# Local attention, norms and gated layers in one block with waits by unit and bank, and retention in rounds of eight heads

## The reference

```
x = x + 0.5 * moe(layernorm(x))            # L0_ffn, 8 experts, top 1
x = x + attention(layernorm(x))            # L0_attn, 16 heads of 8, softmax
x = x + 0.5 * moe(layernorm(x))
x = x + 0.5 * L1_ffn(layernorm(x))         # two layers, below
x = x + retention(layernorm(x))            # L1_attn, 16 heads of 8
x = x + 0.5 * L1_ffn(layernorm(x))

# one of the two layers of L1_ffn; shift_token moves channels 64..127 by one token
x = x + local_attention(shift_token(x) @ wqkv) @ wo     # 8 heads of 64, window 64
h = layernorm(shift_token(x)) * lg + lb
h = h @ w1 + b1;  a, g = split(h)
x = x + (a * gelu(g)) @ w2 + b2

# retention: no softmax, a decay mask instead
qk = (q k^T) / sqrt(8) * decay * (t >= s);  out = qk v;  group norm by head;  out @ Wo
```

## Time and profile before

| | |
|---|---|
| runs | 2715.57, 2727.88, 2728.41 us; median 2727.88 us |
| profiled execution | 2716.49 us, its span 2714.5 us |
| busy, share of the span | PE 90%, ACT 67%, DVE 66%, POOL 59%, PEld 63% |
| mean granted TensorE clock | 0.943 of full |

### The profile page before, as it was taken

The page is one execution under the profiler, slowest core; times in us unless marked ns, Lnnn a source line. Parts: engine busy times, 40 slices in busy tenths (PEclk is TensorE's granted clock), DMA queues, the critical chain, the costliest instruction groups (busy, mean ns, idle before and its releaser), DMA issues. The chain is left out here.

```text
span 2714.5 us, 65721 instructions
## 1 busy us (share of the span) xinstructions
PE 2442.9 (90%) x21430; PEld 1699.6 (63%) x21430; DVE 1801.2 (66%) x3884; ACT 1831.2 (67%) x6004; POOL 1604.8 (59%) x1534
## 2 busy tenths in 40 slices
PE   5596999994797999988999988998899989999988
PEld 3593666653794777735777734774677754677753
DVE  2494888862584888845888743564788863788854
ACT  2254888872345999945999943225899972899972
POOL 2672777753673888814888811220788860888850
PEclk7797999996898999999999998899999999999999
DMA  6111000000112000000000000000000000000000
GB/s 263 46 48 37 2 0 0 0 1 20 45 45 79 1 0 0 0 1 0 1 0 0 0 1 0 1 0 1 1 0 0 0 1 0 2 0 0 0 1 31
DMA packets 20373, 42.71 MB, mean 16 GB/s; under 512 B 4016, under 2 KB 14256, under 8 KB 19472
## 3 DMA queue, kind: packets, MB, share of 16 engines
q1 hardware_dynamic: 15696, 31.71, 3.3%
q0 software_dynamic: 4544, 9.35, 1.0%
HBM read 24.45 MB, written 16.59 MB: 15 GB/s over the span
## 5 line engine op out<-in xcount | busy, mean ns | idle before, releaser
L233 POOL TENSOR_TENSOR la_t<-la_t,la_tS 128x512 f32<-128x512 f32 x256 | 401.5, 1568 | 23.9 <-POOL la_tS L229 7.6
L229 POOL TENSOR_TENSOR la_tS<-la_t,tabs 128x512 f32<-128x512 f32 x256 | 325.9, 1273 | 113.4 <-DVE la_t L316 104.5
L253 ACT ACTIVATE la_pr<-psum,la_nm 128x128 f32<-128x128 f32 x1024 | 361.5, 364 | 42.5 <-DVE la_nm L320 34.5
L315 DVE TENSOR_TENSOR la_t<-psum,tabs 128x512 f32<-128x512 f32 x256 | 176.9, 691 | 215.3 <-POOL la_t L233 179.2
L224 POOL TENSOR_TENSOR la_pr<-la_pr,la_rl 128x512 f32<-128x512 f32 x256 | 266.6, 1041 | 54.0 <-DVE la_rl L310 23.9
L138 PE MATMUL psum<-la_hT,big 128*128 128x256 f32 x1024 | 271.0, 388 | 24.6 <-POOL la_hT L215 13.5
L298 DVE SCALAR_TENSOR_TENSOR la_qk<-la_rn,la_t 128x512 f32<-128x512 f32 x256 | 277.0, 1082 | 9.9 <-ACT la_rn L285 6.9
L778 POOL TENSOR_TENSOR ss_pr<-ss_pr,ss_rl 128x256 f32<-128x256 f32 (+1 forms) x256 | 221.4, 886 | 91.0 <-DVE ss_rl L881 88.9
L157 PE MATMUL psum<-la_sq,cf 128*128 128x512 f32 x512 | 264.6, 599 | 0.0
L824 ACT ACTIVATE ss_pr<-psum,ss_nm 128x128 f32<-128x128 f32 (+1 forms) x512 | 210.6, 444 | 9.2 <-DVE ss_nm L874 9.1
L138 PEld LDWEIGHTS psum<-la_hT,big 128*128 128x128 f32 x1024 | 177.9, 194 | 49.3 <-issue 18.3
(11 more groups left out here) (177 smaller groups left out, 5617.2 us busy)
## 6 DMA issues: line engine op xcount, KB each, us to landing
big<-early SPq DMA_DIRECT2D x1, 6688.0 KB, 38.3
ex_xb<-sorted SPq DMA_DIRECT2D x78, 64.5 KB
z<-token_y SPq DMA_DIRECT2D x16, 256.0 KB, 6.3
sorted<-z SPq DMA_DIRECT2D x2, 1999.5 KB, 19.0
big<-late SPq DMA_DIRECT2D x1, 3114.0 KB, 10.1
cf<-const SPq DMA_DIRECT2D x1, 2089.5 KB, 12.0
x<-x_t SPq DMA_DIRECT2D x4, 512.0 KB, 6.9
x_final<-x SPq DMA_DIRECT2D x1, 2048.0 KB, 6.3
```

Source lines behind the costliest of these rows:

```text
L229: pool.tensor_tensor(tS[:, :], t2[:, :], tab[:, 1, :], ALU.mult).then_inc(ts_ready, 1)
L233: pool.tensor_tensor(t3[:, j % 2, :], t1[:, :], tS[:, :], ALU.add).then_inc(summed, 1)
L253: ins = act.activation(pr[:, (j - 3) % 2, h, t * P:(t + 1) * P], s_ps[h][:, t * P:(t + 1) * P], ACT.Exp, bias=nm[:, (j - 3) % 2, h, t:t + ...
```

## The change

1. `layer_norm`, `local_attention` and `gated_ffn` no longer open a block. They return a `Stage` with one function for each engine and two for waits: `there(eng, s)` waits until unit `s` of the stage's output is written, and `free(eng, bank)` until its last use of a PSUM bank is over. `attended_layers` builds the seven stages and `in_one_block` writes each engine's seven streams one behind the other in one block, with no barrier between them. The other norms go through `norm_alone`, a block for each as before.
2. The first user of a bank, or of a part of z or hn, waits for the stage before by `prev.free` or `prev.there`. `gated_ffn` uses its banks in another order, (4, 5), (6, 7), (0, 1) for up and 2, 3 for down.
3. The shifted norm writes its shifted copy directly into hn and norms it in place; the ring `hb`, the buffer `normed` and their waits are gone. The norm's scratch and Gelu's output lie in the part of `big` that held the experts' weights.
4. The semaphores of all seven stages live until the block ends, and are cleared one by one by SP in the next block (at the end of the program: beside the output's DMA).
5. `retention` goes by two rounds of eight heads for each sequence. A round makes its scores in all four quarters of the array into banks 3 to 6, 512 columns each, and DVE masks them in two instructions of 128x1024. There is one set of score banks: the next scores wait until the last round is masked (`p_ready >= 2 * s`). Projection runs two sequences ahead, values one.

```
-            block = ctx.enter_context(nc.Block())
...
+def in_one_block(nc, past_sems, stages):
+    with nc.Block() as block:
...
+        @block.tensor
+        def _(pe):
+            for st in stages:
+                st.tensor(pe)
...
+                if runs(s, U):
+                    pe.wait_ge(h_ready, b + 1)
+                    if is_first(s):
+                        prev.free(pe, 0)
+                        pe.wait_ge(g.late_loaded, 16)
...
+            if isinstance(b, int) and b < 3:
+                prev.there(pool, b // 2)
...
+    def there(eng, s):
+        eng.wait_ge(z_ready, 2 * s + 2)
+
+    def free(eng, bank):
+        last = ((shuffled, U), (ln_ready, U), (o_ready, U), (p_ready, U), (p_ready, U), (pt_low, U), (pt_high, U), (z_ready, B))
+        eng.wait_ge(*last[bank])
...
-                    if s >= NB:
-                        pool.wait_ge(c_ready, s - NB + 1)
...
+                h = part(dst, s).rearrange("p (b t) -> p b t", b=2)
+                if prev is not None:
+                    prev.there(pool, s)
+                pool.tensor_copy(h[0:64], z[0:64]).then_inc(h_low, 1)
...
+            dve.tensor_tensor(part(dst, u), cb[u % NB], rstd[:, u % NB, :], ALU.mult).then_inc(normed_ready, 1)
+            if gain is not None:
+                dve.wait_ge(normed_ready, u + 1)
+                dve.tensor_scalar(part(dst, u), part(dst, u), gain, bias, ALU.mult, ALU.add).then_inc(done, 1)
...
+    up_bank = ((4, 5), (6, 7), (0, 1))
+    down_bank = (2, 3)
...
+                if runs(s, U):
+                    prev.there(pe, s)
+                    for c, (c0, n) in enumerate(HCH):
+                        if is_first(s):
+                            prev.free(pe, up_bank[c][0])
+                            prev.free(pe, up_bank[c][1])
...
-    s_ps = ((g.bank[3], g.bank[4]), (g.bank[5], g.bank[6]))
-    s_pair = (g.bank_pair3, g.bank_pair5)
+    s_ps = g.bank[3:7]
...
+                    if runs(b, B):
+                        pe.wait_ge(kz_ready, 4 * b + 2 * r + 2)
+                        if at_least(s, 1):
+                            pe.wait_ge(p_ready, 2 * s)
+                        for jl in range(2):
+                            for t in range(2):
+                                cs = slice(jl * T + t * P, jl * T + (t + 1) * P)
+                                for q in range(4):
+                                    rs = slice(32 * q, 32 * q + 32)
+                                    ins = mm(s_ps[q][:, cs], kz[rs, k, 2 * r + jl, t * P:(t + 1) * P], qk[rs, k, t * P:(t + 1) * P],
...
-                        dve.tensor_tensor(pr[:, e % SLOTS, :, :], s_pair[e % 2][:, :, 0:T], g.tri_01.unsqueeze(1).to_broadcast([P, 2, T]), ALU.mult).then_inc(p_ready, 1)
+                        for jl in range(2):
+                            dve.tensor_tensor(pr[:, r, jl, :, :], g.bank_quad3[:, :, jl * T:(jl + 1) * T], g.tri_01.unsqueeze(1).to_broadcast([P, 4, T]), ALU.mult).then_inc(p_ready, 1)
```

More of the change, by code:

```diff
@@ new lines, in tensor @@
+    def tensor(pe):
+        for s in range(U + 1):
+            if s < U:
+                if begin is not None:
+                    arrived(pe, s)
+                if shift:
+                    pe.wait_ge(h_low, s + 1)
+                    pe.wait_ge(h_ready, s + 1)
+                elif prev is not None:
+                    prev.there(pe, s)
+                if s < NB and prev is not None:
+                    prev.free(pe, s)
+                if s >= NB:
+                    pe.wait_ge(normed_ready, s - NB + 1)
+                nc.tensor.matmul(cb[s % NB], center, part(dst if shift else src, s), start=True, stop=True).then_inc(c_ready, 1)
+            u = s - 1
+            if u >= 0:
+                pe.wait_ge(sq_ready, u + 1)
+                if u < NB and prev is not None:
+                    prev.free(pe, NB + u)
+                if u >= NB:
+                    pe.wait_ge(ln_ready, u - NB + 1)
+                nc.tensor.matmul(vb[u % NB], mean, sq[:, u % NB, :], start=True, stop=True).then_inc(var_ready, 1)
@@ new lines, in vector, with there, free @@
+    def vector(dve):
+        for u in range(U):
+            dve.wait_ge(r_ready, u + 1)
+            dve.tensor_tensor(part(dst, u), cb[u % NB], rstd[:, u % NB, :], ALU.mult).then_inc(normed_ready, 1)
+            if gain is not None:
+                dve.wait_ge(normed_ready, u + 1)
+                dve.tensor_scalar(part(dst, u), part(dst, u), gain, bias, ALU.mult, ALU.add).then_inc(done, 1)
+    def there(eng, s):
+        eng.wait_ge(normed_ready if gain is None else done, s + 1)
+    def free(eng, bank):
+        if bank < NB:
+            eng.wait_ge(normed_ready, U - NB + bank + 1)
+        else:
+            eng.wait_ge(ln_ready, U - 2 * NB + bank + 1)
@@ L502, in gated_ffn @@
-def gated_ffn(nc, g, layer, last):
+        norm = layer_norm(nc, g, sem, norm_room(ctx, nc, g), src, dst, center, mean, gain=gain, bias=bias, begin=begin)
+        in_one_block(nc, past_sems, [norm])
+def gated_ffn(nc, g, sem, room, layer, last, prev):
     W = 2 * T
@@ new lines, in attended_layers @@
+        room = {k: sb(k, v) for k, v in shapes.items()}
+        at = 0
+        for k, n in (("norm_sq", 4), ("norm_lnv", 2), ("norm_rstd", 4), ("gl", len(HCH))):
+            room[k] = g.big_rest[:, at:at + n * W].rearrange("p (a n) -> p a n", a=n)
+            at += n * W
+        stages = [layer_norm(nc, g, of("first"), room, g.x, g.z, g.center, g.mean, load=late)]
+        for l in range(2):
+            stages.append(local_attention(nc, g, of(f"att{l}"), room, l, stages[-1]))
+            stages.append(layer_norm(nc, g, of(f"norm{l}"), room, g.z, g.hn, g.center, g.mean, shift=True,
+                                     gain=g.l1_gain[:, l:l + 1], bias=g.l1_bias[:, l:l + 1], prev=stages[-1]))
+            stages.append(gated_ffn(nc, g, of(f"gated{l}"), room, l, l == 1, stages[-1]))
@@ L1029, in _ @@
             project(0)
             values(0)
-            keys_by_token(0, 0)
-            state(0)
+            project(1)
             rounds(pe, 1, B // 2 - 1, 2, body)
```

882 lines of the change are left out of this document (428 added, 454 removed).

## The result

The changed kernel takes 2618.49 us (median of 4 runs, 2617.03 to 2621.16), the kernel before 2721.73 (4 runs, 2705.85 to 2728.41): a ratio of 0.9643 with a 95% interval of 0.9618 to 0.9669, about 100 us less. The forecast was 2638, the range 2605 to 2690. The profiled executions took 2621.16 and 2716.49, their spans 2619.4 and 2714.5, so 95.1 us lie between the two traces.

A forecast was written before the change was run, and what follows sets the result against it. PE was taken to bound retention (DVE close behind), attentions and gated layers, with waits at twelve joints. Boundaries 50 us plus retention 34 made 84, off 2716.5 and 2727.9: 2632.5 and 2643.9, forecast 2638 us, range 2605 to 2690.

The forecast's parts named there:

- the main case: Whole kernel: boundaries save 50 us and retention 34, giving 2638 us; own range 2610 to 2665; 76 in 100.
- Boundaries: Joints between stages of both chains: removed waits save 25.3 us a chain, 50 in all, bounds 10 and 65.
- Steps 1 and 4: Joints norm to attention and gated layer to attention, once a chain each: earlier starts save 2.9 and 2.8 us.
- Rival B: Joints: waits on a stage's last unit may replace the barrier, so boundaries give only 10 us; 2672 us; 5 in 100.
- the bound of 10: Joints, bound from below: waits take over each barrier's role and only the branches go, saving some 10 us.
- Clears: Program end: 94 semaphore clears by SP, estimated 5.4 us, hidden beside the output DMA's 5.6 us wait; nothing lost.
- Retention: Retention stage: shorter sequences, with half clock lasting until 1721.3 as before, end it at 1820 instead of 1853.7; saves 34 us.
- The sum that was given for a clock never at half: Retention stage: if the clock were never at half, the change would save 50 us.
- A sequence: Retention at full clock: two rounds of 3.99 and about 3.7 us, 7.7 instead of 9.9; bounds 7.3 and 9.
- the 0.2 of pipeline fill: Retention's scores: a round takes about 1.12 us, twice 0.67 less the pipeline's fill of 0.2.
- Rival A: Retention: PE's waits for DVE keep the clock at half throughout, sixteen sequences of 12.5 us; 2693 us; 10 in 100.
- Rivals C and D: Retention: C, one bank set serializes, no gain, 2666 us, 5 in 100; D, also half clock throughout, 2751, 4 in 100.

## Why the prediction was right, and where not

**Direction and mechanism** were right, and the main case came in: both parts gained. The sum was 84 us, and the two traces have 98 in the places that it names: 4 less than forecast at the joints, 18 more in retention. That the two errors pull in opposite ways is luck.

**Boundaries, 50 us forecast, 46 measured.** By the ends of stages, counted from the first norm's start, in the four or two places of each kind: attention to the end of the shifted norm saved 4.5, 2.9, 4.1, 4.6 (forecast 4.5); shifted norm's end to the end of the gated layer 5.6, 5.4, 5.4, 5.6 (5.3); norm to the end of attention 1.4 and 2.8 (2.9); gated layer to the end of the next attention 1.8 and 2.2 (2.8). Steps 1 and 4 were somewhat too high: an attention that starts sooner does not end as much sooner, since its first units wait for one another as before. The matmuls of the first chain's norm took 16.5 us and not 15.0 in the profile after, the 1.5 that is missing in its 1.4. The 2.9 among the first four is clock too: PEclk before was 0.91 from the end of the attention to the norm's last product in the other three places, 3.4 us at half in each, and 1.00 in this one, where 1.2 to 1.7 less was there to be saved. After the change it is 1.00 and 14.76 us, to 0.01, in all four. So the 4.5 that I read from one joint held for the three joints whose clock had fallen in the same place. The first two joints before (busy PE, PEld, DVE, ACT, POOL, then PEclk):

```profile
1164.91:1184.17 19.26, 16.46 (x33) 6.15 (x32) 6.63 (x11) 12.93 (x22) 9.96 (x17) 0.91 0.00 0
1566.58:1584.25 17.67, 14.87 (x33) 5.50 (x32) 6.87 (x11) 12.94 (x22) 10.08 (x17) 1.00 0.01 1
```

**Rival B** feared waits that stand for a stage's last unit, as the barrier did. The run with whole stages is that case, and in it little is gained: barriers and branches are worth 3.5 us over both chains (818.6 and 819.1 from a chain's first to last matmul, where it was 819.9 and 821.3), less than the bound of 10. The change waits by unit, and that gave the rest.

**Clears** went nearly as worked out: 5.7 us beside the DMA where 5.4 stood, 0.9 of the DMA's wait left, the end 0.8 us longer than before.

**Retention, 34 us forecast, 52 measured: the term that was off** is "If the slow stretch lasts as before until 1721.3". I carried a stretch of the old stage over to one with other groups. It ended at 1663.8. By the prices measured, 0.34 to 0.41 for each us at half, the 38 us less make 13 to 15 of the 18 that were missing. The sum that was given for a clock never at half, 50, was the near one. The 12.5 for a sequence at half stays untested: less than one sequence ran there. Nor does a run show why the clock rises so early, beyond that the new retention has it behind either chain.

**A sequence, 7.7 forecast, 7.49 measured**, 3.4 us in all, the rest of the gap. Scores (1.10 from start to start) and PV (1.01) were sized right, masks at 1220 ns to the nanosecond, so the slope from 425 and 689 held. No row before shows the 0.2 of pipeline fill in the scores' term; twice the old 0.67 less the measured 1.10 leaves 0.24. Too high was the state: with its product 0.54 from start to start (1684.93 to 1685.47) where 0.79 stood, and 0.22 alone where 0.46 stood. So PE's first round is 3.74 and not 3.99, level with the chain at 3.75. DVE's masks stand in that step with 2.36 once and with 2.43 in the next; two start to start take 2.36.

**Rival A** (half clock all through) had it the wrong way round. At full clock PE is busy less of the time than before, 103.8 of 117.9 us, waits on DVE once a sequence for 0.66, and its clock stays full. The Trainium skill (TensorE: Matmul & The Clock Gate, section A second HAM failure mode: psum-queue depth-cycling) tells of a kernel in which short idling between groups made the clock oscillate. This stage does not show it; the run with four quarters in the old units, where PE was busy 125 of 165 us behind the first stretch and the clock fell four times more, agrees with it.

**Rivals C and D** needed the single set of banks to put everything in series. Scores and masks are in series, but PV, projection and state fit beside the masks. That alternating banks do carry the old form is seen where they were taken from it: 10.5 us a sequence.

The Trainium skill (TensorE: Matmul & The Clock Gate, section Measured speedup vs the span model) gives 3.07 times for four row tiles, with 512 columns. The estimate of 1.5 for a round's scores that I made from it was too high, since 32 records in four quarters took 1.17. But the figure itself is not refuted, as I had it: my 0.71 and 0.74 compare two quarters with four. With one quarter after the other the same 32 records took 2.79, so four in turn gain 2.4 times at 128 columns.

## What to carry to other kernels

Between two stages that walk the same units, let each engine wait for the unit and the bank it needs: here the barrier cost some 0.3 us and waiting for the last unit 1.4 to 5.6 each time, part of it by the clock that falls in the wait. Where a stage starts with PE waiting, look at the granted clock behind the start, not at PE's busy share: here the low clock outlasted the wait by 39 us (1682.0 to 1721.3), and a few idle full-size matmuls gave its price, where no wait followed. And never carry a stretch at half clock over into the forecast of a stage whose matmuls are grouped anew: give both ends.

## What was unexpected of the hardware

- A half clock that was entered at the start lasted 48 and 65 us in two executions of the same code (in the first PE was busy for all of the last 39.5), 27 us behind another chain, and 3.4 us with six idle matmuls ahead. In the second it came back for 10 us after 14 us in which PE was busy for 13.44. The kernel before varied by 37 us between runs (2700.09 to 2737.32), along with its mean clock (0.951 to 0.933).
- The same score matmuls, issued over the quarters in turn instead of quarter by quarter, took 1.17 us a round and not 2.79, shortened a sequence from 10.7 to 7.5 us, and kept the clock up behind the start, where it fell four times otherwise.
